# Skip term, softplus and summed half-states of a selective-scan block rearranged between VectorE, ScalarE, GpSimd and DMA

## The reference

```python
xr, z = split(xm @ W_in)
u = silu(causal_conv4(xr) + b_conv)
dt, Bm, Cm = split(u @ W_x)                       # 64, 16, 16
delta = softplus(dt @ W_dt + b_dt)
A = -exp(A_log)
for t in range(T):                                # h: DI x N, starts at 0
    h = exp(delta[t][:, None] * A) * h + (delta[t] * u[t])[:, None] * Bm[t][None, :]
    y[t] = sum(h * Cm[t][None, :], axis=-1)
out = ((y + u * D_param) * silu(z)) @ W_out
```

## Time and profile before

| | |
|---|---|
| median of 3 runs | 3898.7 us (3895.74 to 3901.77) |
| the profiled execution, its own time | 3902.06 us |
| its span in the trace | 3899.8 us |
| granted PE clock, mean | 0.909 |
| busy share PE, DVE, ACT, POOL | 86%, 69%, 52%, 49% |
| first scan | at 1584.19 us of the span |
| last scan | at 3790.61 us of the span |

### The profile page before, as it was taken

The page is one execution under the profiler, slowest core; times in us unless marked ns, Lnnn a source line. Parts: engine busy times, 40 slices in busy tenths (PEclk is TensorE's granted clock), DMA queues, the critical chain, the costliest instruction groups (busy, mean ns, idle before and its releaser), DMA issues.

```text
span 3899.8 us, 36422 instructions
## 1 busy us (share of the span) xinstructions
PE 3364.2 (86%) x12362; PEld 1765.7 (45%) x12362; DVE 2700.1 (69%) x3429; ACT 2043.9 (52%) x3517; POOL 1906.8 (49%) x1147
## 2 busy tenths in 40 slices
PE   7899999999999997668888888888888888888758
PEld 3344444444444433444444444444444444544443
DVE  3253534444353533689898998998998998998981
ACT  2233434343433434746756756756766676676632
POOL 0121221212221221867767757767857867767661
PEclk9999999999999998668998998998998988988859
DMA  5101011010101011012132231232221221221111
GB/s 175 68 1 46 1 46 41 6 46 1 46 1 46 1 76 40 30 52 77 57 111 76 65 129 53 89 111 66 81 98 65 85 94 65 84 98 65 49 62 43
DMA packets 106361, 238.43 MB, mean 61 GB/s; under 512 B 10609, under 2 KB 10721, under 8 KB 103106
## 3 DMA queue, kind: packets, MB, share of 16 engines
q1 hardware_dynamic: 101314, 226.73, 17.1%
q0 software_dynamic: 2304, 8.39, 1.1%
q10 hardware_dynamic: 2560, 0.98, 0.1%
HBM read 193.85 MB, written 33.83 MB: 58 GB/s over the span
## 4 chain that ended last, share of the span: by engine, by line
PE 23%; DVE 21%; ACT 9%; issue 7%; POOL 2%; DMA 0%; POOLq 0%; SPq 0%; DVEq 0%; ACTq 0%
PE bank L1559 12%; DVE HS L1433 9%; DVE acc L1442 8%; PE bank L1574 5%; PE bank L1639 4%; ACT bank L1255 3%; POOL HS L1167 1%; DVE U L1474 1%; PE bank L1637 1%; PE bank L1627 1%; ACT U L1317 1%; PE bank L1583 1%; DVE G L1462 1%; ACT G L1371 1%; ACT L1318 0%
## 5 line engine op out<-in xcount | busy, mean ns | idle before, releaser
L1167 POOL TENSOR_TENSOR HS<-DU,brep 128x1024 f32<-128x1024 f32 x512 | 1198.9, 2363 | 445.0 <-PE bank L1574 443.7
L1433 DVE TENSOR_TENSOR_SCAN HS<-bank,HS 128x1024 f32<-128x1024 f32 x512 | 1168.1, 2284 | 88.7 <-ACT bank L1255 81.0
L1574 PE MATMUL bank<-ident,HS 128*128 128x128 f32 x4096 | 678.9, 317 | 297.9 <-DVE acc L1442 251.5
L1255 ACT ACTIVATE bank<-delta,aneg 128x511 f32<-128x511 f32 x1024 | 662.0, 681 | 410.3 <-DVE HS L1433 409.3
L354 POOL TENSOR_TENSOR PR<-PR,rrec 128x512 f32<-128x512 f32 x256 | 260.0, 1039 | 1160.3 <-DVE rrec L612 1160.3
L1574 PEld LDWEIGHTS bank<-ident,HS 128*128 128x128 f32 x4096 | 555.9, 163 | 574.2 <-DVE HS L1433 324.6
L1442 DVE SCALAR_TENSOR_TENSOR acc<-bank,C,acc 128x512 f32<-128x512 f32 x928 | 647.0, 741 | 101.3 <-PE bank L1574 98.1
L1559 PE MATMUL bank<-XM,w_l 128*128 128x512 f32 x1024 | 509.3, 639 | 54.9 <-DVE U L1474 32.4
L1559 PE MATMUL bank<-w_l,G 128*128 128x512 f32 x1024 | 471.1, 605 | 10.8 <-ACT G L1371 10.8
L441 ACT ACTIVATE PR<-bank,nsmax 128x512 f32<-128x512 f32 x256 | 173.4, 682 | 374.6 <-DVE nsmax L608 374.6
L714 PE MATMUL bank<-w_l,NT 128*128 128x512 f32 x768 | 344.7, 597 | 4.8 <-ACT NT L393 4.8
(11 more groups left out here) (172 smaller groups left out, 3884.4 us busy)
## 6 DMA issues: line engine op xcount, KB each, us to landing
brep<-b_d SPq DMA_DIRECT2D x256, 256.0 KB, 3.2
w_l<-in_L_cond_W_in SPq DMA_DIRECT2D x14, 2048.0 KB, 10.8
w_l<-in_L_cond_W_full SPq DMA_DIRECT2D x8, 2048.0 KB, 8.6
w_l<-in_L_cond_W_out SPq DMA_DIRECT2D x7, 2048.0 KB, 9.0
X<-in_x SPq DMA_DIRECT2D x8, 1024.0 KB, 5.3
x_d<-X SPq DMA_DIRECT2D x8, 1024.0 KB, 4.6
xm_d<-XM SPq DMA_DIRECT2D x8, 1024.0 KB, 3.9
ot_d<-OT SPq DMA_DIRECT2D x8, 1024.0 KB, 5.8
```

The costliest lines, as they stand in the source:

```text
L1167: nc.gpsimd.tensor_tensor(HS[:, u % DEEP], DU[:, chunks(j, s), :], brep[:, m % 3, :].unsqueeze(1).to_broadcast([P, UC, T]), ALU.mult).then ...
L1255: last = nc.scalar.activation(dA[:, s, i, 1:T], delta[:, c, 1:T], ACT.Exp, scale=aneg[:, c, n:n + 1])
L1433: nc.vector.tensor_tensor_scan(h, dA[:, u % 2].rearrange("p i t -> p (i t)"), h, 0.0, ALU.mult, ALU.add).then_inc(scanned, 1)
L1574: last = nc.tensor.transpose(y_bank[t % 2][:, i * P:(i + 1) * P], h, ident[:])
```

## The change

Five things, the last being a new set of slot numbers:

1. `total` on DVE keeps one operation a chunk instead of two: y * silu(z). The skip term is prepared apart: ACT makes u * D (into DU for chunks 0 to 3, whose DU is used up by then, into G for 4 to 7), POOL multiplies it by silu(z) (`gate_skip`) and, once DVE has written its product, adds the two (`add_skip`). PE may reuse a y bank after that one operation (`tot_done` in place of `g_done`), and each pair of chunks of the W_out product waits only for its own chunks.
2. Softplus is one activation a chunk, in pairs between two table loads; POOL keeps only delta * u (`step_times_input`).
3. SPARED goes from state 10 of the first half to states 3, 6, 9 of the first and 4, 6, 9 of the second: 6 of 32 half-states of a batch. The scratch is a tile of its own, `terms`.
4. Waits that the old scratch and the old correction needed go (`load_xm`, the z-product's copy, `attention`).
5. The slot tables.

```diff
-        SPARED = ((10,), ())
+        SPARED = ((3, 6, 9), (4, 6, 9))
-        PE_P = ((29, 29), (30, 31), (31, 32), (32, 32))
-        PE_O = ((2, 2, 2, 3), (5, 5, 5, 5), (14, 15, 15, 15), (21, 21, 22, 22))
+        PE_P = ((29, 29), (29, 30), (31, 31), (33, 33))
+        PE_O = ((2, 2, 2, 3), (5, 5, 5, 7), (14, 15, 15, 15), (21, 21, 22, 22))
-        SP_B, SP_OUT, SP_OT, SP_GATE, SP_XM, SP_PROJ, SP_FULL = 18, 13, 15, 26, 23, 26, 0
+        SP_B, SP_OUT, SP_OT, SP_GATE, SP_XM, SP_PROJ, SP_FULL = 13, 13, 27, 21, 13, 25, 5
...
         def window(j, n):
-            later = [m for m in SPARED[j % 2] if m > n]
-            return (later[0], later[0] + 1) if later else (n + 2, n + 2)
+            return n + 2, n + 2 + (n + 2 in SPARED[j % 2])
...
+                def step_times_input(n, c):
                     pool.wait_ge(*ring.done(n, f"dt{c}"))
-                    nc.gpsimd.tensor_tensor(delta[:, c, :], DU[:, c, :], delta[:, c, :], ALU.add).then_inc(delta_done, 1)
-                    pool.wait_ge(delta_done, i + 1)
-                    pool.wait_ge(u_done, i + 1)
+                    pool.wait_ge(u_done, n * IC + c + 1)
                     nc.gpsimd.tensor_tensor(DU[:, c, :], delta[:, c, :], U[:, c, :], ALU.mult).then_inc(du_done, 1)
+                def gate_skip(b, c):
+                    i = b * IC + c
+                    pool.wait_ge(ud_done, i + 1)
+                    pool.wait_ge(z_done, i + 1)
+                    y = (DU if c < HC else G)[:, c, :]
+                    nc.gpsimd.tensor_tensor(y, y, zs(b, c), ALU.mult).then_inc(skip_done, 1)
+                def add_skip(b, c):
+                    i = b * IC + c
+                    pool.wait_ge(skip_done, i + 1)
+                    pool.wait_ge(tot_done, i + 1)
+                    nc.gpsimd.tensor_tensor(G[:, c, :], G[:, c, :], DU[:, c, :] if c < HC else zs(b, c), ALU.add).then_inc(g_done, 1)
...
+                def softplus(n, pair):
+                    act.preload_act_table_set(SOFTPLUS)
                     for c in pair:
-                        after(act, dbu_done, (2 * (n - 1) + c // HC + 1) * UNITS)
-                        nc.scalar.activation(DU[:, c, :], e_abs[:, c % HC, :], ACT.Ln, bias=1.0).then_inc(sp_ln, 1)
+                        act.wait_ge(ring.full, ring.at(n, f"dt{c}"))
+                        after(act, dA_done, (2 * n + c // HC - 1) * UNITS)
+                        nc.scalar.activation(delta[:, c, :], ring.bank(n, f"dt{c}")[:], ACT.Softplus, bias=col("L1_cond_b_dt", c)).then_inc(ring.emptied["act"], 1)
                     act.preload_act_table_set(EXP_AND_LN)
...
                         c = q * HC + i
                         if q == 0 and b:
                             dve.wait_ge(ring.full, ring.at(b - 1, "f3"))
+                        if q == 1:
+                            dve.wait_ge(skip_done, b * IC + c + 1)
                         dve.wait_ge(z_done, b * IC + c + 1)
-                        dve.wait_ge(tot_done, j * HC + i + 1)
-                        nc.vector.tensor_tensor(G[:, c, :], y_bank[i % 2][:], zs(b, c), ALU.mult).then_inc(g_done, 1)
+                        dve.wait_ge(yt_full, j * TURNED + N * TT + i + 1)
+                        nc.vector.tensor_tensor(zs(b, c) if q else G[:, c, :], y_bank[i % 2][:], zs(b, c), ALU.mult).then_inc(tot_done, 1)
```

185 lines of the change are left out of this document (65 added, 120 removed).

## The result

The changed kernel takes 3849.89 us (median of 4 runs, 3849.43 to 3851.6), the kernel before 3898.7 (three runs; with a fourth, of 18016.46 us, left in, the median is 3900.23): the ratio is 0.9874 (95% interval 0.9862 to 0.9886), about 49 us gained. The forecast was 3806, a gain of 93; its sign held and so did its outer range, 3750 to 3862, but not its own range of 3775 to 3838, and its size was near twice what came.

The account below looks back on a forecast made before the run. DVE was taken as the likely bound, with PE and PE-DVE round trips setting the pace around the change of half. Terms of 10.25 us a batch, 82.0 over eight, plus 11.25 made 93.2: 3806 us, range 3750 to 3862.

Parts of the forecast that it names:

- a: Five more spared half-states a batch, each taking two steps' additions off DVE, 2.6 us: +13.0 us a batch.
- d: First half: state 6, beside PE's products in slots 12 to 15, -1.5 us; state 3, behind W_out products, -0.6.
- b: State 6 of the second half, inside ACT's silu(u) groups: scan 1.25 us later, DVE's 2.6 idle, -3.85 a batch.
- e: Total at the start of a second half, on DVE: four of eight operations stay, +2.6 us a batch.
- f: Total at the start of a first half, on PE's chain: 8.35 us becomes about 5.7; together +3.3 a batch.
- i: Heads' load moves from slot 15 to 27, behind the projection weights: PE waits 0 to 4 us, -1.0 a batch.
- h: Twelve transfers a batch instead of two, landing in time by 0.2 us: -0.5 a batch.
- the ends: Start before the first scan, first and last halves, last total, one batch change fewer: 11.25 us in all.
- slower by late transfers: Rival (0.06): DVE waits for landings; gain used up at 1.0 us a transfer on average, 4013 us at 2.2 each.
- Step c: State 9 of the second half, between two softplus pairs: ACT needs 15.0 us against DVE's 12.8, -2.2.
- Step g: Softplus's correction leaves POOL, for which ACT's copies of z waited 9.3 us a batch: +1.0, between 0 and 3.
- second rival: Stalls are larger (0.16): change of half stays as it is, each stall a half longer, 3879 us.

Follow-up runs that it names:

- the kernel with only state 10: The changed kernel with its spared half-states back to state 10 of the first half alone, all else as changed: 3888.54 us, 0.9978 of the kernel before.

## Why the prediction was right in its sign and too large in its size

What held, by the steps of the prediction. **a and d:** against the kernel with only state 10, states 3 and 9 of the first half and 4 of the second gave 2.5 to 2.6 us each (the 0.6 allowed against state 3 was not needed), state 6 of the first half 1.0 with 1.1 forecast. **b:** the scan waited 4.23 us, and slots 12 to 16 of the second half took 1.2 more than before, with 1.25 forecast (-3.85 against the 2.6 of a). (Its 0.15 us "after DVE was free" is the step of 3.65 against the usual 3.50; by the rows the additions end at 2623.90 and the scan starts 0.06 later.) Without state 6 they give the 1.2 back, but its whole price was 3.2 a batch (26 us): the step of slot 17, where DVE waits for its transfer, falls by 1.5, and those of slots 22 and 25 by 2.5 and 1.5, further than b looked. (The kernel with only state 10 takes 1.1 more there too, though it spares nothing in that half; that part isn't explained, so the match of 1.2 with 1.25 may be chance.) **e, f and i:** 4.9 a batch forecast (2.6 + 3.3 - 1.0); the change of batch gave 2.3, and slot 30 of the first half to slot 11 of the second 6.1, of which 2.6 belong to state 4: 5.8 together. The chain of step f takes 5.74 us with about 5.7 forecast, and the projection's eight product instructions behind it 0.46 us each. **The start:** first scan 1579 forecast, 1578.0 measured.

What was luck. **The sum of a to d with h** was 42 us in the forecast and 41 by the kernel with only state 10, but not by its terms. In the traces of these two kernels the first seven batches gain 6.7 us each, where 4.35 were forecast, and the last batch loses 2.9 and the first scan 1.3, where the ends were to bring 7.5. Of the gain a batch, 2.1 us lie in slots 20 to 29 of the first half, where the kernel with only state 10 waits for its own late transfer, which no term has. And h, forecast at 0.5, cost 3.1.

What failed. The prediction had 10.25 a batch and 11.25 at the ends; the four batches measured gained 5.45 each, which makes 43.6, and the rest 5.4.

**Step h** is the largest. It said "So it fits by 0.2 us" and took 0.5 us a batch with bounds of 0 and 2.2 a transfer. The transfers cost 3.1 a batch and 14 us in the last batch. Two things were wrong in it. The landing was read from 16 transfers at one place, 15 of which had no load of SP's beside them; at the new places half have one, and land later (last section). And the issue was counted with POOL as free as at state 10, while in slots 20 to 22 of the second half it is behind, with a product and two drives ahead of it. A third was not in the step at all: ACT too waits, for the scratch tile that the transfer still reads, 8.05 us in the last second half. The rival "slower by late transfers" had the right mechanism; at 36 to 41 us over 96 transfers the price is about 0.4 us each, below the 1.0 from which it decides.

**Step c** had state 9 of the second half worth 0.4 us a batch, 3 in all, before its transfers. With them it cost 3 us, or 10 where state 6 is not spared, which is little against the uncertainty. The scans do wait in slots 20 to 22 (batches 3 to 6), but 1.3 to 2.2 us for a late drive, up to 0.5 for ACT in slot 21, and 1.9 to 4.5 for ACT in slot 22, behind a copy of z that waits for PE. The step had reckoned with softplus and scalings alone.

**Step g** is another. It took +1.0 a batch from ACT's wait for POOL's correction. Softplus as one function in the kernel before took the wait away and gave 0.3 us a batch in slots 29 and 30, where the additions wait for PE's turn instead; the 3.2 more in slot 21 come from where that experiment put a pair.

**What no step priced** are the new slot tables in the saturated slots. The prediction went through the places where operations come or go, and took the rest of the tables as neutral. In the kernel with only state 10, slots 12 to 29 of the first half and 12 to 25 of the second take 7.7 us a batch more than before; DVE's wait for the late second transfer of state 10 is 2.7 to 3.9 us of it, and the load of W_in that stands beside that transfer is an entry of the new tables; the rest is not divided further. I have not tried single entries of the tables beyond those above, nor the skip term on POOL alone, so which of them costs this stays open.

**Step i** was mis-sized: -1.0 a batch, and moving the load back gave 14 us, 1.8. The forecast said that PE would wait 0 to 4 us and it waited 1.75.

The two ways of dividing, leaving out the transfers (41 us) and leaving out the sparing (41 us), overlap, because each run also changes what the other engines wait for. No run gives a single split of the missing 44 us.

**The ends:** the last second half, free of silu and softplus, was to give 6.05; it gained 8.2 in the whole last batch against 5.45 in a usual one, because its transfers took 14 back.

Of the signs that the prediction named, steps of 2.2 us at states 3, 9 and 4 came, and the waits for ACT in slots 12 to 14. "Additions waiting under 10 us in all for the transfer" was wrong, 46.4, and so was "a period near 271", 276.2. Of the three signs that the forecast is wrong, one came: the projection's first product waits for the heads. Additions wait on the transfer in 26 cases of 96, not in most, and PE's clock is 0.94 over a period, not under 0.90. The result lies by the side of the second rival, "about 3842 if only one of the two happens"; the stalls were larger, though not where that rival put them, and the change of half did gain.

## What to carry to other kernels

A transfer that replaces an engine's addition has a deadline made of three parts, when its issuing engine is free, how long it takes to land, and when the tile it reads is wanted again. Check each at every slot where one will stand, and what else is being loaded at that moment, since one example at a quiet place says nothing on the others. Before crediting the removal of a wait, ask what else would have released that instruction: three times here (the correction in slots 29 and 30, the copy of tile 0, the copy of z-product 3) the wait removed uncovered another of about the same length. When one edit spares work at several places, time each by leaving it out: here one of six cost 26 us and one brought nothing. A sum that comes out right is no proof of its terms: compare slot by slot.
